# The score and row matmuls of an attention loop, each split over the four column tiles of the array

## What is computed

```
xn = _layernorm(x, axis=-1)
x = x + attention(xn, ...) + feed_forward(xn, ...)

# attention: q, k, v by bitnet_linear (signs of the weights, times a scale)
scores = jnp.einsum('bhqd,bhkd->bhqk', q, k) / np.sqrt(HEAD_DIM)
attn = jax.nn.softmax(scores, axis=-1)
out = jnp.einsum('bhqk,bhkd->bhqd', attn, v)
...
# feed-forward: silu(x @ gate.T) * (x @ up.T) @ down.T with ternary weights
```

## Time and profile before

| | |
|---|---|
| median of 3 runs | 501.98 us (500.68 to 502.21) |
| the profiled execution | 501.71 us, span 500.0 us |
| granted TensorE clock, mean | 0.997 |
| busy, share of the span: PE, DVE, ACT | 96%, 83%, 70% |
| attention loop on DVE | 159.1 to 399.3 us |

### The profile page before, as it was taken

One profiled execution on the slowest core, in us unless ns is written; L12 is line 12 of the kernel. 1 busy time (PEld: TensorE's weight loads), 2 busy tenths in 40 slices (PEclk: granted clock), 3 DMA queues, 4 the chain that ended last, 5 costly groups with the idle time before them and its releaser, 6 DMA issues.

```text
span 500.0 us, 10314 instructions
## 1 busy us (share of the span) xinstructions
PE 480.1 (96%) x4171; PEld 163.6 (33%) x4171; DVE 415.7 (83%) x487; ACT 348.1 (70%) x640; POOL 101.7 (20%) x154
## 2 busy tenths in 40 slices
PE   1899999999998999999999999999999999999996
PEld 0564444433332222222222222222222233333442
DVE  7879868676777999999999999999999955223986
ACT  1943543352228999999999999999999978774000
POOL 4212334534424011011011011001101213241021
PEclk9999999999998999999999999999999999999999
DMA  8853783642103812212212312222221133453321
GB/s 263 266 109 84 165 163 41 182 93 24 22 0 40 152 25 42 64 25 43 64 24 44 65 39 47 43 55 34 42 64 25 15 108 94 102 156 86 105 83 45
DMA packets 64424, 39.28 MB, mean 79 GB/s; under 512 B 39729, under 2 KB 53937, under 8 KB 64377
## 3 DMA queue, kind: packets, MB, share of 16 engines
q1 hardware_dynamic: 55352, 27.59, 22.6%
q0 software_dynamic: 8304, 10.95, 11.8%
q10 hardware_dynamic: 720, 0.08, 0.1%
HBM read 33.37 MB, written 10.48 MB: 88 GB/s over the span
## 4 chain that ended last, share of the span: by engine, by line
PE 93%; DVE 3%; ACT 2%; DMA 1%; issue 1%; SPq 0%; ACTq 0%; DVEq 0%
PE ps L1309 28%; PE ps L1144 19%; PE ps L1247 14%; PE ps L1153 11%; PE ps L1217 5%; PE ps L1204 5%; PE ps L1125 4%; PE ps L1339 3%; PE ps L1278 2%; ACT room L718 2%; DMA hlo<-x 1%; DVE stats L777 1%; DVE room L799 1%; PE ps L1117 1%; DVE room L804 0%
## 5 line engine op out<-in xcount | busy, mean ns | idle before, releaser
L853 DVE TENSOR_REDUCE nmx<-ps 128x1 f32<-128x1024 f32 x248 | 283.2, 1216 | 13.4 <-PE ps L1153 13.2
L718 ACT ACTIVATE room<-ps 128x512 f32<-128x512 f32 x512 | 271.1, 598 | 20.5 <-PE ps L1278 11.5
L1309 PE MATMUL ps<-room,vcur 128*32 128x256 f32 (+1 forms) x1880 | 159.8, 412 | 0.3 <-ACT room L718 0.3
L1153 PE MATMUL ps<-kA,qst 48*128 48x512 f16 x496 | 139.3, 384 | 0.0
L1247 PE MATMUL ps<-qst,kB 50*128 50x512 f16 x432 | 134.8, 384 | 1.3 <-ACT room L718 1.3
L1144 PE MATMUL ps<-room,wf 128*128 128x512 f16 x448 | 100.6, 379 | 0.0
L1309 PEld LDWEIGHTS ps<-room,vcur 128*32 128x32 f32 x1880 | 37.2, 108 | 95.0 <-issue 52.1
L699 ACT ACTIVATE room<-ps,gsc 128x512 f32<-128x512 f32 x28 | 19.2, 686 | 62.4 <-PE ps L1144 62.4
L1144 PEld LDWEIGHTS ps<-room,wf 128*128 128x128 f16 x448 | 42.4, 98 | 55.1 <-issue 7.2
L1247 PEld LDWEIGHTS ps<-qst,kB 50*128 50x128 f16 x432 | 28.3, 93 | 97.0 <-ACT room L718 84.6
L562 POOL TENSOR_SCALAR mxs<-mxs 16x128 f32<-16x128 f32 x16 | 8.3, 520 | 214.8 <-DMA mxs<-m_scratch 214.6
(11 more groups left out here) (137 smaller groups left out, 316.9 us busy)
## 6 DMA issues: line engine op xcount, KB each, us to landing
qst<-q_scratch SPq DMA_DIRECT2D x32, 192.0 KB, 3.6
o_scratch<-osb SPq DMA_DIRECT2D x16, 256.0 KB, 2.5
q_scratch<-parts SPq DMA_DIRECT2D x12, 256.0 KB
hlo<-x SPq DMA_DIRECT2D x8, 256.0 KB, 5.3
parts<-x POOLq DMA_DIRECT2D x8, 256.0 KB, 3.7
wf<-gate POOLq DMA_DIRECT2D x14, 128.0 KB, 3.8
wf<-up POOLq DMA_DIRECT2D x14, 128.0 KB, 5.9
wd<-down POOLq DMA_DIRECT2D x1, 1792.0 KB, 13.9
```

What stands on the lines that cost most here:

```text
L718: nc.scalar.activation(probs[:, s % 2, r, :], ps[:, bank_of(step, i), :], ACT.Exp, scale=gam_reg[par][r]).then_inc(scores_free, 1)
L853: nc.vector.tensor_reduce(nmx[:, hf, idx:idx + 1], bank_pair(idx % 2), AX.X, ALU.max, negate=True).then_inc(rows_free, 1)
L1153: return nc.tensor.matmul(ps[:, 2 * (idx % 2) + b, :], qst[low:low + KROWS, par, hf, head, qt * P:(qt + 1) * P], kA[low:low + KROWS, par, ...
L1309: mm = nc.tensor.matmul(ps[32 * r:32 * r + 32, value_bank(step_ // TT), of], vcur[:, par, key_tile(r, j), :], probs[:, s % 2, r, of], star ...
```

## The change

Every score of `scores` and every row half that `scores` issues becomes four matmuls of 32 stationary columns (strips), each on one of the four column tiles, with the same 512 moving columns. The stationary operand is cut into columns 0 to 31, 32 to 63, 64 to 95 and 96 to 127, and each strip writes 32 partitions of the bank that the one matmul wrote before. Semaphores are raised by the last strip alone, and waited for ahead of the first. The row maxima ahead of the loop (`rows`) pass a width of 128 and stay as they were, and so does `late_scores`.

```diff
-            def half_rows(par, hf, idx, b):
+            def half_rows(par, hf, idx, b, width=32):
 
                 head, qt = idx // (HALF // P), idx % (HALF // P)
                 low = b * HI
-                return nc.tensor.matmul(ps[:, 2 * (idx % 2) + b, :],
-                                        qst[low:low + KROWS, par, hf, head, qt * P:(qt + 1) * P],
-                                        kA[low:low + KROWS, par, :], start=True, stop=True)
+                for c in range(0, P, width):
+                    at_query = qt * P + c
+                    mm = nc.tensor.matmul(ps[c:c + width, 2 * (idx % 2) + b, :],
+                                          qst[low:low + KROWS, par, hf, head, at_query:at_query + width],
+                                          kA[low:low + KROWS, par, :], start=True, stop=True)
+                return mm
 
             def rows(n, par, hf, idx):
                 pe.wait_ge(rows_free, n + 1)
-                half_rows(par, hf, idx, 0)
-                half_rows(par, hf, idx, 1).then_inc(rows_ready, 1)
+                half_rows(par, hf, idx, 0, P)
+                half_rows(par, hf, idx, 1, P).then_inc(rows_ready, 1)
...
-                    nc.tensor.matmul(ps[:, score_bank(block_, e), :],
-                                     kB[low:low + SROWS, par, kt % (TT // 2) * P:(kt % (TT // 2) + 1) * P],
-                                     qst[low:low + SROWS, par, hf, r, :], start=True, stop=True).then_inc(scores_ready, 1)
+                    for c in range(0, P, 32):
+                        at_key = kt % (TT // 2) * P + c
+                        mm = nc.tensor.matmul(ps[c:c + 32, score_bank(block_, e), :], kB[low:low + SROWS, par, at_key:at_key + 32],
+                                              qst[low:low + SROWS, par, hf, r, :], start=True, stop=True)
+                    mm.then_inc(scores_ready, 1)
```

## The result

The changed kernel takes 504.23 us (median of 20 runs, 502.71 to 506.49) against 502.2 us (20 runs, 500.27 to 505.42): a ratio of 1.0043 [1.0028, 1.0058], some 2.2 us slower. The forecast was 7.7 us slower.

What follows compares the result with a forecast made beforehand. DVE paced the loop at 1.132 us a half-step; PE's 1.108 + 0.054 + 0.006 = 1.168 us would exceed it, adding 216 x (1.168 - 1.1324) = 7.7 us to 501.71: 509.4 us. Range 501 to 522; the forecast's own 503 to 522.

Steps and rivals of the forecast that it cites:

- So PE may take 1.132 us for a half-step at no cost: In the loop, DVE paces at 1.132 us; PE takes 1.108, and only what exceeds 1.132 is paid, 216 times.
- The wait for ACT at a block's start falls away, I expect: One score a block waits for ACT, costing PE 0.27 us; expected gone, 3.5 us in all if it stayed.
- The stagger: Strips in the loop start 0.007 us apart, so a half-step of PE grows by a mean of 0.054 us.
- The switch, cost 0: Changing array division between scores/rows and values takes about 0.1 us each way in a half-step; both kept, cost 0.
- Eight tiles side by side: Score strips and row-half strips run eight at once, nothing more; four at once would add 0.43 us a half-step.
- the two slow rivals: In the loop, TensorE's instruction intake limits (547 us, 0.12 with everything 522 to 560), or no side-by-side (590 us, 0.04).
- the 56 of that rival: TensorE cannot take instructions fast enough: 56 ns per load-matmul pair, half-step 1.34 us, 547 us; chance 0.12 (522 to 560).
- The weight loads: Twelve more loads in a half-step of the loop: taken as 0.006 us, at worst about 0.05 us.
- Faster: Rival: PE delivers earlier at the loop's two ends, where DVE waits 2.1 us; 499.6 us could come out, chance 0.04.
- the signs to look for: Loop: DVE waits in most half-steps; scores start every 1.17 us; scores and rows take about 0.59 us, values 0.57.
- A piece of DVE still unbroken at 1.132 us would make the forecast wrong: Sign in the loop's row maxima: their unbroken piece should be gone; if it stayed at 1.132 us, the forecast fails.

Runs made afterwards that it cites:

- Experiment 1: The changed kernel with one line of score_bank different, a block's first six scores taking banks own, one, two, own, one, two: 501.89 us, ratio 0.9985.
- experiment 3: The changed kernel with the loop's row halves streaming 448 of 512 keys, so its output is not the layer's: 501.10 us, ratio 0.9976.
- experiment 8: The kernel before, with strips of 32 columns only in the scores and row halves of late_scores: 501.52 us, ratio 0.9984.
- experiment 9: The changed kernel with strips of scores and row halves contracting over all 128 rows, so its output is not the layer's: 543.43 us (one run).
- experiment 6: The changed kernel with strips of a score and of the row half beside it issued by turns: 505.84 us, ratio 1.0076.
- experiment 7: The changed kernel with only the loop's scores in strips of 32 columns, row halves of 128 columns as before: 621.18 us (one run).
- experiment 5: The changed kernel with two strips of 64 columns in place of four of 32: 502.42 us, ratio 1.0007.

## Why the prediction was off

The direction was right and the size was not: 2.2 us for 7.7. Two errors pulled against each other, and the direction was luck: the reason given for it, a PE that needs more than DVE's 1.132 us, did not come about (1.127), and by the prediction's own rule the measured pace would have cost nothing.

**"So PE may take 1.132 us for a half-step at no cost"** failed. It holds for a half-step without a wait. One half-step in 16 lasts 1.42 us, and PE must win that back in the other 15, so its limit was (18.10 - 1.42) / 15 = 1.112 us, of which it used 1.108. The prediction had read that PE catches up (rows 4) and did not ask how much faster it must be to do so. Experiment 1 shortens the wait and 1.127 is nearly free; experiment 3 goes to 1.10 and the whole wait is free.

**"The wait for ACT at a block's start falls away, I expect"** failed for the same reason. It was read as arrears of ACT, which a slower PE would clear. It is a chain: two scores, two exponentials, and the bank of the second is wanted two scores later. A slower PE does not shorten it (0.28 us after, 0.27 before), another order of banks does (1). That ACT would have no arrears was right, and the wait stayed without them. Its cost had been bounded, at 3.5 us if it stayed, and that bound was nearer the mark than the term taken.

**The stagger** was right as a mechanism and mis-sized: 0.019 us for 0.054. Two figures in it were wrong. Strips of 64 rows start some 3 ns apart, not 7: in experiment 8 all 16 loads of the late scores take 0.14 us, and one takes 0.09, which is 0.05 / 15 = 3.3 ns; the eight strips that start at 0.226 to 0.249 us after the first give the same. The 7 ns of rows 7 come from strips of 128 rows, and those of experiment 9, of that shape too, start 34, 7 and 7 ns after one another: the number was taken from another shape. The Trainium skill's 4 ns for a tile, cited in the prediction from "TensorE: Matmul & The Clock Gate", "The mechanism", is nearer to what was measured. And the strips do not wait for their place in the program (the half-step from 250.85 above, and experiment 6), so that the last of the second eight is never held up behind a whole first row half: with eight at 3.3 ns it starts 0.023 us behind the first of them, and nothing comes on top. The second pair of before starts 0.003 us apart in the trace, so 0.020 us are added, and 0.019 were measured. The same section of the Trainium skill says that matmuls start strictly in the order of the program; the traces of the change and of experiment 6 show another order of starts, and the measurement decides.

**The switch, cost 0**, was right: 0.31 us from the last strips to the values (249.97 to 250.28) as before (250.41 to 250.72), and experiments 8 and 9 show that with alike columns the rows alone make it. **Eight tiles side by side** was right, and with it the two slow rivals fell: 24 pairs of a load and a matmul in 1.127 us are 47 ns a pair on average, under the 56 of that rival. **The weight loads** (0.006) can't be told apart from the stagger; together they are 0.019. **Faster** did not come: DVE's waits at the loop's ends are 0.55, 0.87 and 0.71 us, 2.13 where there were 2.1.

Of the signs to look for, DVE waits in one half-step of 16 and not in most, scores start every 1.13 us and not 1.17, and scores and rows take 0.55 us and not 0.59; only the values' 0.57 came as said. The last sign was wrong as a sign. "A piece of DVE still unbroken at 1.132 us would make the forecast wrong": the piece looked unbroken at 1.146 us, and held idle times too short to break it, such as the 0.13 us above. Its length divided by its count showed them; its being unbroken did not.

No kernel here that computes the layer beats the one before. The kernel before, the change with another order of banks, and the shorter strips all stand at DVE's 18.10 us a block or just above.

## What to carry to other kernels

An engine that runs a little ahead of the bound spends its lead on its own rare waits: its limit is worked out over a whole period, waits included, and not over the step without one. A wait for a buffer that recurs at one place is looked up in the order of buffers before it is called arrears, since arrears go away with a slower producer and a chain does not. And a matmul split over column tiles is nearly free if all that runs beside it is split in the same way (0.019 us in 1.108), while one left wide beside it costs a switch each time (621 us).

## What the runs showed of the hardware

- Matmuls on different tiles can start against the order of the program, in the order in which tiles come free (the half-step of the change from 250.85, and experiment 6). Their semaphores are raised in the order of the program all the same: in that half-step the score's at 251.51 us and the row half's, which had started first, at 251.57. No run shows what this does beyond four groups of four strips.
- Tiles of 32 and of 128 columns do not run side by side, even in opposite halves of the array's rows: they follow each other, 0.32 us from start to start (experiment 7). Other pairs of shapes were not tried.
- At the loop's start PE is idle for 1.28 us, waiting for ACT, and behind it the granted clock differs from run to run. The stretch of 156 to 159 us of the change: busy time of PE, PEld, DVE, ACT and POOL, then the granted clock, DMA share and GB/s.

```profile
156.00:159.00 3.00, 2.95 (x48) 0.77 (x48) 2.30 (x2) 2.38 (x5) 2.43 (x3) 0.62 0.00 0
```

The same stretch with strips of 64 columns (experiment 5):

```profile
156.00:159.00 3.00, 3.00 (x44) 0.89 (x40) 2.71 (x3) 3.00 (x7) 2.84 (x4) 1.00 0.31 2
```

Part of the first stretch runs at the level of 1.2 GHz, none of the second; the profiled run of the kernel before has 0.53 in the same stretch. The values at 157.54 us take 1.08 us in the one, those at 156.78 us 0.64 in the other, and the first block takes 20.60 and 19.21 us. That is 1.4 us, more than half of what the change costs, and it lies ahead of anything that the change does to a block: a difference of this size is read from the middle of the loop and from many runs, not from one profile.
